# The edge stage of a graph-attention kernel: nine products and nine additions in each of the last eight turns with logits, and one turn without logits at the end instead of two

## The chip, the cores and the metric

The kernel runs on one core of a Trainium2 chip. A core has five engines, each with its own stream of instructions: TensorE (PE, whose weight loads are listed as PEld), VectorE (DVE), ScalarE (ACT), GpSimd (POOL) and SyncE (SP). They meet only at semaphores. The metric is the device time of one execution in microseconds (us); lower is better. A q behind an engine's name (DVEq) stands for its sequencer, which handles register loads and semaphore waits and hands the rest to the engine.

## What is computed

One layer on 6250 nodes of 256 features: a layer norm, graph attention with 8 heads over 100000 edges sorted by destination, a residual, then a second norm and a mixture of 16 experts (top 2). The change touches only the attention's sum over edges:

```
h = jnp.einsum('ni,hio->hno', x, W)
attn_src = jnp.einsum('hno,ho->hn', h, a_src[..., 0])
attn_dst = jnp.einsum('hno,ho->hn', h, a_dst[..., 0])
edge_attn = jax.nn.leaky_relu(attn_src[:, src] + attn_dst[:, dst], negative_slope=0.2)
edge_attn_exp = jnp.exp(edge_attn - jnp.max(edge_attn))
attn_sum = jax.ops.segment_sum(edge_attn_exp.T, dst, num_segments=N)
attn_norm = edge_attn_exp / (attn_sum[dst].T + 1e-10)
weighted_h = attn_norm[..., None] * h[:, src]
out = jax.ops.segment_sum(weighted_h.transpose(1, 0, 2), dst, num_segments=N)
```

## The kernel before

There are four stages. The first norms the nodes, projects them and stores rows of 264 numbers (256 features and 8 source logits) in `node_rows`. The second is the edge stage, from about 100 to 1194 us. The third divides by the sums, adds the residual, norms again and routes tokens to experts. The fourth runs the experts and the last norm.

In the edge stage the edges lie in 832 steps of up to 128 edges, each step's edges within one tile of 128 destination nodes. Eight steps are a group (`GROUP`), so there are 104 groups (`GROUPS`). For each step POOL issues one indirect gather of 128 rows of `node_rows` (L773), into one of four slots of eight steps. Everything else of the stage is a software pipeline in turns, `for g in range(GROUPS + 2)`, which PE and DVE each write out in their own program:

- In a turn g below 104 ("with logits") DVE forms the logits of group g: it sums four parts of the destination logits that PE put into a bank (`edge_logits_sum`, L1311), adds the gathered source logits once the group's rows have landed (`edge_logits_add`, L1318: the z addition), applies the slope, and takes a maximum over heads and steps (L1329, `zmax`). PE transposes `zmax` (L935), DVE reduces it and updates the running maximum (L1334, L1336), PE spreads that over the partitions (L942), and ACT negates it, takes the exponentials and builds the one-hot matrices of the group's destinations. DVE then multiplies the gathered rows by them in four quarters (`weigh`, L1344).
- In a turn g from 2 on, PE forms the eight products of group g - 2 (`aggregate`, L917: a transposed one-hot times 128 rows of 264), each into one of five banks, and DVE adds each product to its tile's rows in SBUF (`add_step`, L1358; for a group's first step L1356, which also scales by `fall`). The product of step k waits for addition k - 5 (`acc_add`), and addition k waits for product k (`agg_mm`) and addition k - 1.

So turns 104 and 105 have no logits; they only sum groups 102 and 103. In turn 104 DVE also prepares the epsilons of the division (`tile_max`, L1370 to L1380), PE spreads them (L957), and in turn 105 DVE copies them out (L1383). The next stage's first instruction on DVE is L1424.

The tile of a step is data, so DVE and PE load eight tile numbers per turn into registers (`tiles_of`, one TENSOR_LOAD at L418). DVE does it at the head of its turn, ahead of `edge_logits_sum`.

## Time and profile before

| | |
|---|---|
| time before, median of 3 runs | 1827.97 us (1824.74 to 1829.16) |
| the profiled execution's own time | 1831.03 us |
| its span from first to last instruction | 1828.2 us |
| granted TensorE clock, mean over the span | 0.83 of full |
| busy: PE, DVE, ACT, POOL | 75%, 64%, 41%, 67% |
| idle of POOL before the gathers (L773) | 288.5 us, of it 219.9 us "issue" |
| last gather issued | 1167.7 us |

The span is that of one execution under the profiler, and its own time lies 2.8 us above it and 3.1 us above the median. All starts below count from the span's first instruction. In the rows "idle before" is the time for which the engine had nothing to do ahead of an instruction, and the name behind the arrow is what the profile takes for the cause of its end. "issue" means that no semaphore accounts for it.

### The profile page before, as it was taken

The numbers are of one execution on the slowest core, as the hardware profiler recorded it, in microseconds if no ns is written. First come the engines' busy times: TensorE is split into PE (matmuls) and PEld (weight loads), VectorE is DVE, ScalarE is ACT, GpSimd is POOL, SyncE is SP. The second block draws the span as 40 slices with busy tenths as digits, with TensorE's granted clock in tenths as the row PEclk, the third lists the DMA queues.
The fourth block names the chain that finished last, engine by engine and source line by source line (L and its number), as shares of the span: only waits on it lengthen the run. The fifth ranks groups of instructions, "written<-read, shape, count | busy, mean of one in ns | idle before, by whom it ended". The sixth has DMA issues, their size and how long they took to land. (4 is left out here: it accounts for less than half of the span.)

```text
span 1828.2 us, 28107 instructions
## 1 busy us (share of the span) xinstructions
PE 1376.6 (75%) x6723; PEld 1059.3 (58%) x6723; DVE 1178.4 (64%) x3565; ACT 752.0 (41%) x2240; POOL 1233.2 (67%) x1237
## 2 busy tenths in 40 slices
PE   4926767767677667767667777757689999999965
PEld 3714444444444444444444444446579999999953
DVE  6757777777777777777777777689834443333346
ACT  2624444545444444445444454434323333333335
POOL 1267777777777777777777777426547767656746
PEclk9958888888878888787788887755589999999977
DMA  7344444444444444444444444265468878888874
GB/s 230 120 136 134 130 134 130 133 130 136 129 133 134 131 132 130 135 128 133 128 127 135 130 135 136 63 218 179 117 194 225 212 205 216 215 204 206 214 187 165
DMA packets 167984, 283.80 MB, mean 155 GB/s; under 512 B 33294, under 2 KB 94822, under 8 KB 167670
## 3 DMA queue, kind: packets, MB, share of 16 engines
q0 software_dynamic: 62256, 143.99, 31.7%
q1 hardware_dynamic: 102466, 137.18, 24.1%
q10 hardware_dynamic: 3108, 0.85, 0.2%
q8 instruction: 64, 1.05, 0.2%
q14 instruction: 90, 0.74, 0.2%
HBM read 240.57 MB, written 42.16 MB: 155 GB/s over the span
## 5 line engine op out<-in xcount | busy, mean ns | idle before, releaser
L773 POOL DMA_INDIRECT region<-node_rows,region x832 | 818.3, 984 | 288.5 <-issue 219.9
L917 PE MATMUL bank<-region 128*128 128x264 f32 x1664 | 599.8, 508 | 0.7 <-DVE region L1356 0.3
L1358 DVE TENSOR_TENSOR region<-region,bank 128x264 f32 x728 | 311.0, 427 | 222.2 <-PE bank L917 209.2
L917 PEld LDWEIGHTS bank<-region 128*128 128x128 f32 x1664 | 377.5, 244 | 69.3 <-DVE region L1344 0.7
L1344 DVE TENSOR_TENSOR region<-region 128x512 f32<-128x512 f32 x416 | 285.2, 687 | 3.1 <-ACT region L645 3.1
L631 ACT ACTIVATE region<-iota_row,region 128x128 f32<-128x128 f32 x832 | 262.5, 386 | 0.0
L935 PE MATMUL bank<-ident,zmax 128*1 128x128 f32 x104 | 33.0, 318 | 301.8 <-DVE zmax L1329 301.8
L641 ACT ACTIVATE neg_max<-bank 128x1 f32<-128x1 f32 x104 | 17.8, 171 | 584.5 <-PE bank L942 584.5
L705 ACT ACTIVATE region<-bank,b_col 128x128 f32<-128x128 f32 x452 | 129.5, 368 | 306.9 <-PE bank L1050 304.2
L833 POOL DMA_INDIRECT sum_rows<-region,row_u x113 | 179.4, 1587 | 107.6 <-DVE region L1709 43.8
L1050 PEld LDWEIGHTS bank<-region 128*128 128x128 f32 x1808 | 221.2, 193 | 6.2 <-DVE region L1666 0.5
L1050 PE MATMUL bank<-region 128*128 128x128 f32 x1808 | 221.9, 276 | 0.1
L1062 PE MATMUL bank<-region 128*128 x904 | 214.1, 380 | 0.5 <-DVE region L1709 0.5
L935 PEld LDWEIGHTS bank<-ident,zmax 128*1 128x1 f32 x104 | 8.2, 79 | 348.3 <-DVE zmax L1329 348.3
L1062 PEld LDWEIGHTS bank<-region 128*128 128x128 f32 x904 | 162.9, 190 | 18.8 <-issue 1.2
L636 ACT ACTIVATE region<-region,ones 128x512 f32<-128x512 f32 x208 | 150.1, 722 | 6.8
L806 POOL DMA_INDIRECT region<-y_rows,token_u x113 | 112.4, 994 | 51.1 <-issue 24.7
L1709 DVE SCALAR_TENSOR_TENSOR region<-bank,region 128x256 f32<-128x256 f32 x113 | 54.6, 484 | 139.5 <-PE bank L1062 78.5
L1666 DVE COPY region<-bank 128x256 f32<-128x256 f32 x113 | 47.8, 423 | 124.2 <-PE bank L1039 124.2
L565 ACT ACTIVATE region<-bank 128x256 f32<-128x256 f32 (+4 forms) x182 | 65.5, 380 | 97.6 <-PE bank L980 42.1
L905 PE MATMUL bank<-attn_parts,region 128*128 x832 | 95.2, 187 | 0.6
L942 PEld LDWEIGHTS bank<-run_max,ones 1*128 1x128 f32 x208 | 47.2, 281 | 69.1 <-DVE run_max L1336 69.1
(239 smaller groups left out, 1550.1 us busy)
## 6 DMA issues: line engine op xcount, KB each, us to landing
region<-in_L_ffn_w SPq DMA_DIRECT2D x129, 512.0 KB, 5.0
region<-dloc_rows SPq DMA_DIRECT2D x104, 256.0 KB, 3.4
region<-node_rows,region POOLq DMA_INDIRECT x832
node_rows<-region SPq DMA_DIRECT2D x12, 528.0 KB, 3.1
y_rows<-region SPq DMA_DIRECT2D x7, 896.0 KB, 5.9
sum_rows<-region SPq DMA_DIRECT2D x7, 896.0 KB, 7.5
region<-in_x SPq DMA_DIRECT2D x6, 896.0 KB, 10.5
region<-sum_rows SPq DMA_DIRECT2D x5, 896.0 KB, 11.1
```

What stands on the lines that cost most here:

```text
L631: ins = s.activation(onehot[:, slot + j, :], iota_row[:, :], ACT.Square, bias=dloc[:, k:k + 1], scale=-1.0)
L636: s.activation(four, four, ACT.Relu, bias=ones[:, 0:1], scale=-1.0).then_inc(onehot_ok)
L705: ins = s.activation(hidt_buf[:, j % 2, f * P:(f + 1) * P], bank[HIDT_BANKS[j % 2]][:, f * P:(f + 1) * P], ACT.Relu, bias=flat_b1[:, bass. ...
L773: p.indirect_dma_start(gathered[g % SLOTS][:, j, :], None, node_rows, bass.IndirectOffsetOnAxis(src_idx[:, k:k + 1], 0)).then_inc(row_in[g ...
L806: p.indirect_dma_start(xg_buf[:, j % XG, :], None, y0_rows, bass.IndirectOffsetOnAxis(token_u[:, j:j + 1], 0)).then_inc(xg_in[j % XG], 16)
L833: p.indirect_dma_start(sum_rows, bass.IndirectOffsetOnAxis(row_u[:, j:j + 1], 0), y_buf[:, j % 3, :], None, compute_op=ALU.add).then_inc(y ...
L905: ins = pe.matmul(z_bank(g)[:, j * AD:(j + 1) * AD], onehot_t[:, g % 2, j, :], flat_parts[:, bass.ds(tiles[j] * AD, AD)], start=False, sto ...
L917: pe.matmul(bank[AGG_BANKS[k % AGG]][:, 0:ROW], onehot[:, (g % 3) * GROUP + j, :], gathered[g % SLOTS][:, j, :], start=True, stop=True).th ...
L1050: ins = pe.matmul(bank[HIDT_BANKS[j % 2]][:, f * P:(f + 1) * P], w1_buf[:, j % W1_SLOTS, c * HIDDEN + f * P:c * HIDDEN + (f + 1) * P], xgt ...
L1062: ins = pe.matmul(bank[Y_BANKS[j % 2]][:, 0:F_IN], hidt_buf[:, j % 2, f * P:(f + 1) * P], w2_sb[:, bass.ds(expert * (FC * F_IN) + f * F_IN ...
L1344: v.tensor_tensor(hv, hv, pv, ALU.mult).then_inc(weigh_ok)
L1358: v.tensor_tensor(rows, rows, new, ALU.add).then_inc(acc_add)
```

## The change

The steps are no longer tied to turns by `(g - 2) * GROUP`. A function `first_sum(g)` says where a turn begins: up to turn 95 as before, then one step further ahead with each of the turns 96 to 103, so that these eight turns take nine steps each, and turn 104 takes group 103. Turn 105 is gone. PE's `aggregate` and DVE's `add_step` now take step numbers. On DVE the additions come from a generator, `sums(g)`, which loads the tile numbers when its first addition is asked for, and once more for the ninth. The ninth addition stands behind the fourth quarter of `weigh`. `tile_max(3)` stands behind the seventh addition of turn 104 instead of the eighth, and `tile_max(4)` behind the last addition of all. Each product of PE names three semaphores instead of two (every fourth one did so before).

```diff
@@ -367,6 +367,15 @@
+
+        CATCH_UP = 8
+
+        def first_sum(g):
+
+            return min(STEPS, max(0, (g - 2) * GROUP + min(max(g - (GROUPS - CATCH_UP), 0), CATCH_UP)))
+
+        def sums_of(g):
+            return range(first_sum(g), first_sum(g + 1))
...
@@ -413,10 +422,10 @@
-        def tiles_of(eng, engine, g):
+        def tiles_of(eng, engine, k, n):
 
             _, tiles = nc.values_load_multi_w_load_instructions(
-                tile_row[0:1, g * GROUP:(g + 1) * GROUP], engines=[engine], min_val=0, max_val=TILES - 1,
+                tile_row[0:1, k:k + n], engines=[engine], min_val=0, max_val=TILES - 1,
                 skip_runtime_bounds_check_because="the value was clamped on chip")
             return tiles
...
-            def aggregate(g, js):
-                for j in js:
-                    k = g * GROUP + j
-                    if j % 4 == 0:
-                        pe.wait_ge(onehot_ok, 2 * g + j // 4 + 1)
-                    pe.wait_ge(weigh_ok, 4 * g + j // 2 + 1)
+            def aggregate(steps):
+                for k in steps:
+                    g, j = k // GROUP, k % GROUP
+                    pe.wait_ge(onehot_ok, k // 4 + 1)
+                    pe.wait_ge(weigh_ok, k // 2 + 1)
                     if k >= AGG:
                         pe.wait_ge(acc_add, k - AGG + 1)
                     pe.matmul(bank[AGG_BANKS[k % AGG]][:, 0:ROW], onehot[:, (g % 3) * GROUP + j, :],
@@ -922,10 +930,10 @@
-            for g in range(GROUPS + 2):
-                now, last, more = g < GROUPS, g >= 2, g + 1 < GROUPS
-                if last:
-                    aggregate(g - 2, range(0, 1))
+            for g in range(GROUPS + 1):
+                now, more = g < GROUPS, g + 1 < GROUPS
+                steps = sums_of(g)
+                aggregate(steps[0:1])
                 if now:
                     pe.wait_ge(zmax_ok, g + 1)
                     if g >= 1:
@@ -933,16 +941,14 @@
                     else:
                         pe.wait_ge(late_step, LATE["late"])
                     pe.transpose(bank[M_BANK][0:1, 0:P], zmax[:, g % 2:g % 2 + 1], ident[:, :]).then_inc(zmax_tr)
-                if last:
-                    aggregate(g - 2, range(1, 4))
+                aggregate(steps[1:4])
                 if now:
                     pe.wait_ge(run_max_ok, g + 1)
                     if g >= 1:
                         pe.wait_ge(neg_max_ok, g)
                     pe.matmul(bank[M_BANK][:, P + 8:P + 9], ones[0:1, :], run_max[:, g + 1:g + 2], start=True,
                               stop=True).then_inc(max_bc)
-                if last:
-                    aggregate(g - 2, range(4, 6))
+                aggregate(steps[4:6])
                 if more:
                     attn_dst_of(g + 1)
                 if g == GROUPS:
@@ -950,8 +956,7 @@
                     pe.wait_ge(gmax_ok, GROUPS)
                     pe.wait_ge(neg_max_ok, GROUPS)
                     pe.transpose(bank[M_BANK][0:1, 0:P], late_min[:, :], ident[:, :]).then_inc(late_mm)
-                if last:
-                    aggregate(g - 2, range(6, GROUP))
+                aggregate(steps[6:])
                 if g == GROUPS:
                     pe.wait_ge(late_step, LATE["eps_row"])
                     pe.matmul(bank[M_BANK][:, 256:256 + TILES], ones[0:1, :], eps_row[:, 0:TILES], start=True,
@@ -1343,8 +1348,8 @@
                 pv = gathered[g % SLOTS][:, js, F_IN:ROW].unsqueeze(3).broadcast_to([P, 2, HEADS, F_OUT])
                 v.tensor_tensor(hv, hv, pv, ALU.mult).then_inc(weigh_ok)
 
-            def add_step(g, j, tile):
-                k = g * GROUP + j
+            def add_step(k, tile):
+                g, j = k // GROUP, k % GROUP
                 if j == 0:
                     v.wait_ge(fall_ok, g + 1)
                 v.wait_ge(agg_mm, k + 1)
@@ -1384,34 +1389,37 @@
                     v.memset(base[:, 0, :], 0.0).then_inc(late_step)
             onehots_t(0)
             late_groups()
-            for g in range(GROUPS + 2):
-                now, last = g < GROUPS, g >= 2
-                tiles = None
-                if last:
-                    if g == 2:
-                        v.wait_ge(acc_zero, 7)
-                        v.wait_ge(table_step, TABLE["tile_row"])
-                    tiles = tiles_of(v, mybir.EngineType.DVE, g - 2)
+            def sums(g):
+
+                steps, tiles = sums_of(g), None
+                for n, k in enumerate(steps):
+                    if n % GROUP == 0:
+                        if k == 0:
+                            v.wait_ge(acc_zero, 7)
+                            v.wait_ge(table_step, TABLE["tile_row"])
+                        tiles = tiles_of(v, mybir.EngineType.DVE, k, min(GROUP, len(steps) - n))
+                    yield add_step(k, tiles[n % GROUP])
+            for g in range(GROUPS + 1):
+                now = g < GROUPS
                 if now:
                     edge_logits_sum(g)
                     edge_logits_add(g)
                     edge_logits_relu(g)
                     edge_logits_max(g)
-                for j in range(GROUP):
-                    if last:
-                        add_step(g - 2, j, tiles[j])
+                adds = sums(g)
+                for j in range(GROUP + 1):
+                    next(adds, None)
                     if now and j == 1:
                         running_max(g)
                     if j == 3 and g + 1 < GROUPS:
                         onehots_t(g + 1)
-                    if now and j >= 4:
+                    if now and 4 <= j < 8:
                         weigh(g, j - 4)
                     if g == GROUPS and j < 3:
                         tile_max(j)
-                    if g == GROUPS and j == 7:
+                    if g == GROUPS and j == 6:
                         tile_max(3)
-                    if g == GROUPS + 1 and j == 1:
-                        tile_max(4)
+            tile_max(4)
```

What this moves on the engines is shown at three places. Line numbers of the changed kernel are 5 to 9 higher here: L427 is the register load, L1361 and L1363 are the additions, L925 is the product.

The first place is DVE at the boundary of two ordinary turns, before. L1344 is the last quarter of `weigh`, L1311 to L1329 are the logits of the next turn, and L1356 is its first addition (ISA rows set up its address).

```order
L1358 TENSOR_TENSOR region<-region,bank 128x264
L1344 TENSOR_TENSOR region<-region 128x2x256
L418 TENSOR_LOAD tile_row
L1311 TENSOR_REDUCE z<-bank 128x64
L1318 TENSOR_TENSOR z<-z,region 128x64
L1323 SCALAR_TENSOR_TENSOR z<-z 128x64
L1329 TENSOR_REDUCE zmax<-z 128x1
L1356 ISA
L1356 SCALAR_TENSOR_TENSOR region<-region,fall,bank 128x264
```

The same boundary in the changed kernel:

```order
L1363 TENSOR_TENSOR region<-region,bank 128x264
L1349 TENSOR_TENSOR region<-region 128x2x256
L1316 TENSOR_REDUCE z<-bank 128x64
L1323 TENSOR_TENSOR z<-z,region 128x64
L1328 SCALAR_TENSOR_TENSOR z<-z 128x64
L1334 TENSOR_REDUCE zmax<-z 128x1
L427 TENSOR_LOAD tile_row
L1361 ISA
L1361 SCALAR_TENSOR_TENSOR region<-region,fall,bank 128x264
```

The load has moved from ahead of the logits to between `zmax` and the first addition. This is so in every turn from 2 to 103, not only in the last eight.

The second place is DVE at the boundary of turns 102 and 103 in the changed kernel, where the ninth addition and its own load stand behind the last quarter of `weigh`.

```order
L1363 TENSOR_TENSOR region<-region,bank 128x264
L1349 TENSOR_TENSOR region<-region 128x2x256
L427 TENSOR_LOAD tile_row
L1363 ISA
L1363 TENSOR_TENSOR region<-region,bank 128x264
L1316 TENSOR_REDUCE z<-bank 128x64
L1323 TENSOR_TENSOR z<-z,region 128x64
```

One addition more stands ahead of the next turn's logits.

The third place is PE from the last turn with logits on, before. L935 and L942 are turn 103's two small steps, L952 transposes `late_min`, and L957 spreads the epsilons; L980 is the next stage.

```order
L935 MATMUL bank<-ident,zmax 1x128
L917 MATMUL bank<-region 128x264 x3
L942 MATMUL bank<-run_max,ones 128x1
L917 MATMUL bank<-region 128x264 x10
L952 MATMUL bank<-ident,late_min 1x128
L917 MATMUL bank<-region 128x264 x2
L957 MATMUL bank<-eps_row,ones 128x49
L917 MATMUL bank<-region 128x264 x8
L980 MATMUL bank<-ident,region 128x128 x4
```

The same in the changed kernel:

```order
L943 MATMUL bank<-ident,zmax 1x128
L925 MATMUL bank<-region 128x264 x3
L949 MATMUL bank<-run_max,ones 128x1
L925 MATMUL bank<-region 128x264 x11
L958 MATMUL bank<-ident,late_min 1x128
L925 MATMUL bank<-region 128x264 x2
L962 MATMUL bank<-eps_row,ones 128x49
L985 MATMUL bank<-ident,region 128x128 x4
```

The eight products behind the epsilons are gone, one product more stands ahead of L958, and the spreading of the epsilons is now PE's last work of the stage.

## Rows read from the trace of the kernel before

**Rows 1.** Instructions on node_rows: durations (ns min/median/max), starts; idle before, by releaser (us, times)

```profile
L773 POOL DMA_INDIRECT region<-node_rows,region x832: 942/946/2137, 97.5 to 1167.7; - x167
...
  issue: 219.9, 722
...
  PE bank L917: 33.2, 109
```

**Rows 2.** Waits from 150 to 1190: who <- whom: us in total, times, longest

```profile
DVE z L1318 <- DMA region<-node_rows,region: 54.7, 84, 2.4
```

**Rows 3.** DVE, z additions of turns 98-101, 103: start, length (us) [idle before]

```profile
1118.91 0.23 DVE L1318 TENSOR_TENSOR z<-z,region 128x64 f32<-128x64 f32 x1 [1.38 <-DMA region<-node_rows,region]
...
1129.55 0.23 DVE L1318 TENSOR_TENSOR z<-z,region 128x64 f32<-128x64 f32 x1
...
1139.16 0.22 DVE L1318 TENSOR_TENSOR z<-z,region 128x64 f32<-128x64 f32 x1 [0.39 <-DMA region<-node_rows,region]
...
1149.92 0.23 DVE L1318 TENSOR_TENSOR z<-z,region 128x64 f32<-128x64 f32 x1
...
1171.80 0.23 DVE L1318 TENSOR_TENSOR z<-z,region 128x64 f32<-128x64 f32 x1 [1.42 <-DMA region<-node_rows,region]
```

**Rows 4.** Timeline of DVE from the end of turn 103 to the next stage

```profile
1179.71 0.42 DVE L1358 TENSOR_TENSOR region<-region,bank 128x264 f32 x1
1180.05 0.69 DVE L1344 TENSOR_TENSOR region<-region 128x512 f32<-128x512 f32 x1
1180.66 0.48 DVE L1356 SCALAR_TENSOR_TENSOR region<-region,fall,bank 128x264 f32 x1
...
1185.55 0.43 DVE L1358 TENSOR_TENSOR region<-region,bank 128x264 f32 x1 [0.21 <-DVE region L1358]
1185.90 0.27 DVE L1380 TENSOR_SCALAR eps_row<-bank 1x128 f32<-1x128 f32 x1
...
1189.43 0.20 DVE L1383 COPY eps_bc<-bank 128x49 f32<-128x49 f32 x1
...
1193.86 0.22 DVE L1424 TENSOR_TENSOR rsum<-region,eps_bc 128x56 f32<-128x56 f32 x1
```

**Rows 5.** Timeline of PE, the broadcast of the epsilons

```profile
1186.22 0.66 PE L957 MATMUL bank<-eps_row,ones 1*128 1x49 f32 x2 [1.12 <-DVE eps_row L1380]
```

**Rows 6.** The register load L418 on DVE: all of them, then one

```profile
L418 DVEq TENSOR_LOAD <-tile_row x104: 593/596/859, 123.9 to 1185.6; - x104
...
L418 DVEq TENSOR_LOAD <-tile_row x1: 593/593/593, 1157.4 to 1157.4; - x1
```

**Rows 7.** Timeline of DVE, the start of turn 102

```profile
1160.47 0.23 DVE L1318 TENSOR_TENSOR z<-z,region 128x64 f32<-128x64 f32 x1 [1.50 <-DMA region<-node_rows,region]
...
1160.99 0.22 DVE L1329 TENSOR_REDUCE zmax<-z 128x1 f32<-128x64 f32 x1
1161.22 0.49 DVE L1356 SCALAR_TENSOR_TENSOR region<-region,fall,bank 128x264 f32 x1
...
1162.73 0.43 DVE L1358 TENSOR_TENSOR region<-region,bank 128x264 f32 x1 [1.02 <-PE bank L917]
```

**Rows 8.** Timeline of DVE, the first two additions of turn 101

```profile
1150.67 0.49 DVE L1356 SCALAR_TENSOR_TENSOR region<-region,fall,bank 128x264 f32 x1
...
1151.64 0.43 DVE L1358 TENSOR_TENSOR region<-region,bank 128x264 f32 x1 [0.48 <-PE bank L917]
```

**Rows 9.** Timeline of DVE, start of turn 88, and the z addition of turn 89

```profile
1015.54 0.23 DVE L1318 TENSOR_TENSOR z<-z,region 128x64 f32<-128x64 f32 x1 [0.29 <-DMA region<-node_rows,region]
...
1016.64 0.49 DVE L1356 SCALAR_TENSOR_TENSOR region<-region,fall,bank 128x264 f32 x1 [0.36 <-issue]
1017.80 0.43 DVE L1358 TENSOR_TENSOR region<-region,bank 128x264 f32 x1 [0.67 <-PE bank L917]
...
1025.73 0.23 DVE L1318 TENSOR_TENSOR z<-z,region 128x64 f32<-128x64 f32 x1 [0.34 <-DMA region<-node_rows,region]
```

**Rows 10.** The semaphore instruction ahead of each product, L916, on PE's sequencer

```profile
L916 PEldq EVENT_SEMAPHORE  x827: 51/51/51, 134.1 to 1190.4; - x166
```

More of the change, by code:

```diff
@@ L900, in attn_dst_of @@
                     pe.wait_ge(z_sum, g - 1)
-                tiles = tiles_of(pe, mybir.EngineType.PE, g)
+                tiles = tiles_of(pe, mybir.EngineType.PE, g * GROUP, GROUP)
                 pe.matmul(z_bank(g), ones_b[:, :], far_row[:, :, :, :].rearrange("a j k h -> a (j k h)"),
```

## Prediction

> **What bounds the kernel now.** I read the gathers first, then DVE's waits, then the timeline at the stage's end. The reader should see that in the edge stage POOL sets the pace, and that behind the last gather DVE sets the end.
>
> The 832 gathers start from 97.5 to 1167.7, one each 1.288 us, so a turn of eight takes 10.30 us. A gather is at work for 946 ns, and the idle time before it is 0.30 us, whether it is put down to "issue" (219.9 / 722) or to PE's products (33.2 / 109) [rows 1]. Had a slot ever come free late, the second kind would be longer. So no gather waited for a product, and an earlier product brings the gathers nothing.
>
> DVE's z addition waits for rows in 84 of some 100 turns, 54.7 us together [rows 2], or 0.55 us a turn. DVE's own work in a turn is thus 10.30 - 0.55 = 9.75 us. This 0.55 us is all that an ordinary turn can take in unseen. What is unused in one turn can't be saved for a later one, but a delay in one is made up in the next ones.
>
> Turn 103 starts with an idle 1.42 us, at 1171.80 [rows 3]: the last rows set that moment. From there on nobody waits for POOL. The fourth quarter of weigh starts at 1180.05, turn 104's additions at 1180.66, and the next stage's L1424 follows without idle time at 1193.86 [rows 4]. All that comes later hangs on that instruction, so what is gained here is gained at the end.
>
> **The change part by part.**
>
> *The end, 1180.66 to 1193.86, now 13.20 us [rows 4].* In its place there will be:
> - The ninth addition of turn 103, in the slot in which turn 104 starts now. The next addition can't start before it is finished: 0.43 us long plus 0.21 us of hand-over, as in the row at 1185.55 [rows 4]. That is 0.64 us.
> - Turn 104's eight additions with the same steps of tile_max between them: from the first to the eighth 1185.55 - 1180.66 = 4.89 us [rows 4]. PE may run four products ahead, and its rows of group 103 were weighed a turn ago, so I let the spacing stand.
> - The epsilons. L1380 starts 0.35 us after the addition ahead of it (1185.90 - 1185.55) [rows 4], which is now the seventh, 0.64 us ahead of the eighth. PE's broadcast starts 0.32 us later and lasts 0.66 us (1186.22) [rows 5]. The copy takes 0.20 us [rows 4]. I estimate 0.1 us for each of the two hand-overs behind these. From the seventh addition to L1424 that makes 0.35 + 0.32 + 0.66 + 0.1 + 0.20 + 0.1 = 1.73 us, or 1.09 us from the eighth. Today the copy at 1189.43 is covered by additions. That cover is gone, and this is its price.
>
> That is 0.64 + 4.89 + 1.09 = 6.62 us in place of 13.20: **6.58 us saved.**
>
> *The register load, moved in every turn.* Today it stands behind the fourth quarter of weigh: the load at 1157.4 takes 0.593 us beside DVE's running work [rows 6] and costs nothing. In the new place it starts when zmax has been handed to DVE, which then holds 0.22 us of work. The first addition follows zmax by 0.23 us today (1160.99, 1161.22) [rows 7]; it can now come 0.6 us later (0.596 median of 104 loads [rows 6], plus a few hundredths). What hides it: the second addition waits for PE's product, whose way starts at zmax and not at the first addition. Needed between the two additions is 0.49 + 0.21 = 0.70 us. Turn 102 has 1162.73 - 1161.22 = 1.51 us, so 0.81 us of cover and no cost [rows 7]. Turn 101 has 1151.64 - 1150.67 = 0.97 us, so 0.27 us of cover, and 0.6 costs 0.35 us [rows 8]. The trace has tried it: in turn 88 the first addition came 0.36 us late, the second 1.16 us behind it, and the turn's work was 1025.73 - 0.34 - 1015.54 = 9.85 us, no more than turn 102's 1171.80 - 1.42 - 1160.47 = 9.91 [rows 3, 7, 9]. Either price fits under 0.55 us a turn. In turn 103, where there is no cover behind, I charge the dearer: **0.35 us lost.** Bounds: 0 to 0.6.
>
> The Trainium skill speaks against this part: its page "Runtime: NRT & Kernel Launch", section Instruction fetch mechanics, gives a TENSOR_LOAD about 200 ns per register even in bulk. Eight registers would by that take 1.6 us, 0.8 more than turn 102's cover, and the sum would be a slower kernel. The load's rows contradict it, and the rows decide.
>
> *The ninth addition and its load in turns 96 to 102.* Behind a quarter of weigh an addition shifts what follows by 0.34 us (1179.71 to 1180.05) [rows 4]; the bound above is the 0.64 of two additions in a row. Its load of one register takes between nothing and the 0.6 us of eight, and runs beside weigh as the load at 1157.4 does. Does this fit? A turn starts at the later of its rows and the end of the turn before. Turn 98's work, 1129.55 - 1118.91 = 10.64, plus 0.34, makes turn 99 start at 1129.89 instead of 1129.55. Turn 99 (9.22 + 0.34 + 0.35) ends at 1139.80, 0.64 late. Turn 100 (10.76 + 0.34) ends at 1150.90, 0.98 late. Turn 101 (9.05 + 0.34 + 0.35) ends at 1160.64, 0.17 late. Turn 102 (9.91 + 0.34) ends at 1170.89, still 0.91 us before the rows of turn 103 [rows 3, 7]. **Cost 0**, with 0.9 us to spare; up to 2 us when the slow turns fall last.
>
> *PE's third wait.* There is one semaphore instruction of 51 ns ahead of each product, 827 in all, the same for products that name two semaphores and for those that name three [rows 10]. The third adds none: 0. At most it would be another 0.05 us in a turn's first product. The ninth product of a turn stands ahead of PE's wait for zmax, so it is hidden.
>
> **Sum:** 6.58 - 0.35 = **6.2 us**. The profiled execution, 1831.03, would become 1824.8 and its span 1822.0. The median of the runs lies 3.1 us under it: 1827.97 - 6.2 = **1821.8 us**, 0.34% faster. About 0.3% (5.5 us, a time of 1822.5) is what a measurement can tell from no change, so the forecast lies barely past it.
>
> **The rivals.**
>
> 1. *DVE late in turn 103.* Nine steps use nearly all the slack of a turn of 10.30 us. If turns like 98 and 100 (10.6 to 10.8 us) are the last ones, two of them with 0.34 more each lose 2 x 0.8 us against POOL (10.76 + 0.34 - 10.30), and only some of the usual 0.55 us can be set against it. For: turns 98 to 101 are such a cluster. Against: turn 102 makes it up with 0.9 to spare. The gain shrinks by 1 to 2 us: 1823 to 1824, within 0.3%.
> 2. *Slower: the load is not hidden.* If the late first addition delays PE's transposition or the whole turn by its full 0.6 us, DVE's work becomes 9.75 + 0.62 = 10.37 > 10.30 and DVE takes the lead. Stepping through all turns as above, with 0.62 in each and 0.34 more in the last ones, makes turn 103 start 12.6 us late: 1821.8 + 12.6 = 1834.4. It is slower by 0.3% once turn 103 is 11.7 us late, that is, from 0.6 us uncovered in every turn. Against it: turn 88. For it: turn 88 was late by 0.36, not 0.6. At 0.4 uncovered, the lag is 1.1 us and the result within 0.3%.
> 3. *The gain is given back or never seen.* The last stretch depends on PE's clock (granted at two levels, and 0.83 on average), and the three runs spread over 4.4 us. A half-clock stretch in turn 104, where products would have to pass additions, costs 1 to 3 us: 1823 to 1825.
> 4. *More than forecast.* PE at full clock through the epsilons saves about 0.3, and the load in turn 103 under cover 0.35; with the scatter of runs, 1819 to 1821.
>
> **How the numbers follow.** The forecast has 0.57, rival 1 0.15, rival 2 0.08 (over half of it slower by more than 0.3%), rival 3 0.12, rival 4 0.08. The forecast's own range is 1820 to 1824, from the bounds 0 to 0.6 for the load and a run's scatter of 1.5 us. To hold 8 in 10 it takes in rival 1 and most of 3 and 4: 1819.0 to 1826.0. Faster by over 0.3%: 0.7 of the forecast and nearly all of rival 4, with a little of 1 and 3, 0.52. Within 0.3%: the rest of these and part of 2, 0.40. Slower: 0.08.
>
> **What would show it.** In the changed kernel's timeline: the last gather near 1168 and turn 103's z addition near 1172, with some idle time ahead of it (step: no lag); the first addition 0.8 us behind zmax instead of 0.23, and the second at most 0.35 us later than before; the ninth addition 0.34 us long in its slot; no second block of eight additions; the copy of the epsilons behind the last addition with about 0.5 us of idle time; the next stage's first instruction 15.8 us after turn 103's z addition instead of 22.06 (1193.86 - 1171.80). The prediction is wrong if the z waits vanish (rival 2), if the z addition of turn 103 has no idle time (rival 1), or if additions in turn 104 wait for products (rival 3).

## The result: 8 us slower, and the profile after

Six runs of each kernel gave a median of 1836.55 us (1831.42 to 1841.31) after the change and 1828.57 us (1824.74 to 1829.86) before it. The ratio is 1.0044 [1.0026, 1.0062]: slower, on the side to which the prediction gave 0.08, 15 us from the predicted time and outside the range of 1819.0 to 1826.0. Two repetitions, on chips where the kernel before took 1828 and 1831 us, gave 1.0043 and 1.0034.

The gathers first, once as the list of all instructions on `node_rows`, once as groups of instructions from 90 to 1190 us (busy us, mean ns | idle before, by releaser):

```profile
L782 POOL DMA_INDIRECT region<-node_rows,region x832: 945/949/2114, 98.0 to 1177.2; - x167
...
L782 POOL DMA_INDIRECT region<-node_rows,region x832 | 826.8, 994 | 288.5 <-issue 221.3 <-DMA node_rows<-region 35.2 <-PE bank L925 32.0
```

The last gather starts 9.5 us later than in [rows 1]. POOL's idle time is the same 288.5 us and its pattern is the same, so the gathers wait no more than before. The gathers themselves take longer: 8.5 us more in all, while the median has hardly moved (949 against 946 ns). The kernel before has this row in the same view:

```profile
L773 POOL DMA_INDIRECT region<-node_rows,region x832 | 818.3, 984 | 288.5 <-issue 219.9 <-DMA node_rows<-region 35.4 <-PE bank L917 33.2
```

A mean of 984 ns over a median of 946 means that some gathers were already much longer than 946 ns before. The prediction read only the median.

Next the z additions of DVE in turns 97 and 99 to 103:

```profile
1117.39 0.23 DVE L1323 TENSOR_TENSOR z<-z,region 128x64 f32<-128x64 f32 x1 [0.44 <-DMA region<-node_rows,region]
...
1140.57 0.22 DVE L1323 TENSOR_TENSOR z<-z,region 128x64 f32<-128x64 f32 x1
...
1151.99 0.23 DVE L1323 TENSOR_TENSOR z<-z,region 128x64 f32<-128x64 f32 x1
...
1162.33 0.23 DVE L1323 TENSOR_TENSOR z<-z,region 128x64 f32<-128x64 f32 x1
...
1173.84 0.23 DVE L1323 TENSOR_TENSOR z<-z,region 128x64 f32<-128x64 f32 x1
...
1185.37 0.23 DVE L1323 TENSOR_TENSOR z<-z,region 128x64 f32<-128x64 f32 x1
```

From turn 98 on none waits for rows, and the turns take 11.4 to 11.6 us instead of 10.3; only turn 100 (1151.99 to 1162.33) takes 10.34. Turn 103 starts 8.2 us after the last gather's start, before it was 1171.80 - 1167.7 = 4.1 [rows 1, 3]. What happens inside turn 102, and the register loads of DVE (all 111; then those of turn 102, of turn 100, and one of a single register):

```profile
1174.36 0.22 DVE L1334 TENSOR_REDUCE zmax<-z 128x1 f32<-128x64 f32 x1
...
1176.47 0.43 DVE L1363 TENSOR_TENSOR region<-region,bank 128x264 f32 x1 [1.88 <-PE bank L925]
```

```profile
L427 DVEq TENSOR_LOAD <-tile_row x111: 308/596/1867, 132.0 to 1195.0; - x111
...
L427 DVEq TENSOR_LOAD <-tile_row x1: 1866/1866/1866, 1174.4 to 1174.4; - x1
...
L427 DVEq TENSOR_LOAD <-tile_row x1: 606/606/606, 1152.5 to 1152.5; - x1
...
L427 DVEq TENSOR_LOAD <-tile_row x1: 308/308/308, 1172.1 to 1172.1; - x1
```

The profile puts the 1.88 us down to PE, but the load that starts at 1174.4 lasts until 1176.3, and the addition behind it starts then. A load of eight registers takes 1.85 to 1.87 us where its first step is 761, 770, 779, 797, 806 or 815, and 0.60 us where it is 752, 788 or 824. The latter are multiples of four; of these only 788, in turn 100, isn't also a multiple of eight. Until turn 96 every first step is one of eight.

In an ordinary turn, here turn 87, the new place of the load does to DVE what the prediction said: the first addition 0.87 us behind `zmax` instead of 0.23, the second 0.70 behind that.

```profile
1011.88 0.22 DVE L1334 TENSOR_REDUCE zmax<-z 128x1 f32<-128x64 f32 x1
1012.75 0.49 DVE L1361 SCALAR_TENSOR_TENSOR region<-region,fall,bank 128x264 f32 x1 [0.65 <-issue]
1013.45 0.43 DVE L1363 TENSOR_TENSOR region<-region,bank 128x264 f32 x1 [0.21 <-PE bank L925]
```

The end of the stage, from the ninth addition of turn 103 on, answers to [rows 4]:

```profile
1195.23 0.42 DVE L1363 TENSOR_TENSOR region<-region,bank 128x264 f32 x1
1195.90 0.49 DVE L1361 SCALAR_TENSOR_TENSOR region<-region,fall,bank 128x264 f32 x1 [0.24 <-PE bank L925]
...
1200.45 0.43 DVE L1363 TENSOR_TENSOR region<-region,bank 128x264 f32 x1
...
1200.93 0.21 DVE L1388 COPY eps_bc<-bank 128x49 f32<-128x49 f32 x1
...
1201.18 0.22 DVE L1432 TENSOR_TENSOR rsum<-region,eps_bc 128x56 f32<-128x56 f32 x1
```

From turn 103's z addition to the next stage it is 1201.18 - 1185.37 = 15.81 us instead of 22.06. The spans then differ thus: 9.5 us until the last gather's start, 8.2 - 4.1 = 4.1 until turn 103, -6.25 in the end stretch, and 2.4 behind it (636.7 against 634.3 us, work that the change doesn't touch; 636.4 and 636.8 in two more profiles of the changed kernel, and 634.7 to 637.8 in the variants below on chips as fast). Together 9.7, as 1837.9 - 1828.2.

### The profile page after: what moved, and what is told of

It reads as the page before. It is cut to its first block and busy times, and to the rows that moved or that the text cites. A ratio compares the mean times of both kernels' runs of the same rounds, so it can differ in the third digit from the quotient of the medians.

```text
span 1837.9 us, 28117 instructions
## 1 busy us (share of the span) xinstructions
PE 1393.5 (76%) x6723; PEld 1068.3 (58%) x6723; DVE 1177.0 (64%) x3565; ACT 751.8 (41%) x2240; POOL 1244.2 (68%) x1237
## 3 DMA queue, kind: packets, MB, share of 16 engines
q8 instruction: 64, 1.05, 0.2%
## 5 line engine op out<-in xcount | busy, mean ns | idle before, releaser
L782 POOL DMA_INDIRECT region<-node_rows,region x832 | 826.8, 994 | 288.5 <-issue 221.3
L925 PE MATMUL bank<-region 128*128 128x264 f32 x1664 | 615.9, 519 | 0.2
L925 PEld LDWEIGHTS bank<-region 128*128 128x128 f32 x1664 | 387.4, 250 | 71.3 <-issue 0.3
L1363 DVE TENSOR_TENSOR region<-region,bank 128x264 f32 x728 | 310.9, 427 | 175.1 <-PE bank L925 152.5
L650 ACT ACTIVATE neg_max<-bank 128x1 f32<-128x1 f32 x104 | 17.8, 171 | 598.6 <-PE bank L949 598.6
L1055 PEld LDWEIGHTS bank<-region 128*128 128x128 f32 x1808 | 220.9, 193 | 6.2 <-DVE region L1674 0.5
L1067 PEld LDWEIGHTS bank<-region 128*128 128x128 f32 x904 | 162.9, 190 | 20.0 <-issue 2.5
L1361 DVE SCALAR_TENSOR_TENSOR region<-region,fall,bank 128x264 f32 x104 | 50.9, 489 | 66.4 <-issue 63.4
```

The source lines that it names most:

```text
L782: p.indirect_dma_start(gathered[g % SLOTS][:, j, :], None, node_rows, bass.IndirectOffsetOnAxis(src_idx[:, k:k + 1], 0)).then_inc(row_in[g ...
L925: pe.matmul(bank[AGG_BANKS[k % AGG]][:, 0:ROW], onehot[:, (g % 3) * GROUP + j, :], gathered[g % SLOTS][:, j, :], start=True, stop=True).th ...
L1055: ins = pe.matmul(bank[HIDT_BANKS[j % 2]][:, f * P:(f + 1) * P], w1_buf[:, j % W1_SLOTS, c * HIDDEN + f * P:c * HIDDEN + (f + 1) * P], xgt ...
L1067: ins = pe.matmul(bank[Y_BANKS[j % 2]][:, 0:F_IN], hidt_buf[:, j % 2, f * P:(f + 1) * P], w2_sb[:, bass.ds(expert * (FC * F_IN) + f * F_IN ...
L1363: v.tensor_tensor(rows, rows, new, ALU.add).then_inc(acc_add)
```

## The experiments

**Theory A:** the load's new place costs time in every turn, and the first steps that are no multiples of four cost time in the last ones; without both the change brings its 6 us. **Rival B:** nine steps in a turn are too many for DVE or PE, whatever the loads do. **Rival C:** one of the two suspects is the whole loss.

### Each suspect alone and both

`load_ahead`: the changed kernel with the load back ahead of the logits; the first steps stay.

```diff
+                tiles = first_tiles(g)
                 if now:
                     edge_logits_sum(g)
...
-                adds = sums(g)
+                adds = sums(g, tiles)
```

`load_by_group`: the changed kernel, but the tile numbers are loaded a whole group of eight at a time, when its first is needed; the place stays.

```diff
+                n = k // GROUP
+                if n not in group_tiles:
+                    group_tiles[n] = tiles_of(v, mybir.EngineType.DVE, n * GROUP, GROUP)
+                return group_tiles[n][k % GROUP]
```

`both`: that, and the groups needed for the turn's first eight steps are loaded ahead of its logits.

```diff
             for g in range(GROUPS + 1):
                 now = g < GROUPS
+                for k in sums_of(g)[:GROUP]:
+                    tile_of(k)
```

`before_moved`: the kernel before, with eight steps a turn, and nothing but the load moved.

```diff
-                if last:
-                    tiles = tiles_of(v, mybir.EngineType.DVE, g - 2)
                 if now:
                     edge_logits_sum(g)
                     edge_logits_add(g)
                     edge_logits_relu(g)
                     edge_logits_max(g)
+                if last:
+                    tiles = tiles_of(v, mybir.EngineType.DVE, g - 2)
```

The first time:

> The changed kernel with its register load back ahead of the logits in every turn; in turns 97 to 103 it still begins at the turn's own first step. Two costs are supposed: the load's place (P) makes the gathers longer, so the last one ends 9.2 us later than before; the load's start (S), off a multiple of four, makes it 1.86 us instead of 0.60 and puts turn 103 another 4.4 us behind its rows. If P holds: last gather back near 1169, time 1828.6 - 6.2 + what S still costs behind weigh (0 to 5) = 1822.4 to 1827.5. Rival (the gathers' delay has another cause: scatter, or PE's third wait): last gather still near 1178, time 1831 to 1836.

> The changed kernel, but DVE loads eight tile numbers per group, always from a multiple of eight, at the group's first addition; in ordinary turns that is the same place as in the changed kernel. If S holds: every load 0.6 us, turn 103 no longer late against its rows, 4.4 us less than the changed kernel's 1836.5: about 1832. P stays, so the last gather stays near 1178. Rival (the lag at turn 103 comes from the ninth addition, not from the load): no change from 1836.5.

> The kernel before with one thing changed: the register load stands between zmax and the first addition, always eight from a multiple of eight. If P holds: weigh falls differently against the gathers, the last gather ends some 3 to 9 us later, time 1831.5 to 1838. Rival (place costs nothing, as I predicted): 1828.6 within 1.5.

> The changed kernel with loads of whole groups, ahead of the logits: both supposed costs gone, the nine additions and the missing turn kept. If P and S are all that was wrong: the predicted gain, 1828.6 - 6.6 = 1822.0 (1820.5 to 1824). If nine steps a turn cost something of their own: 1825 or more.

Measured: 1.0022 [1.0009, 1.0034], 0.9974 [0.9958, 0.9989], 0.9990 [0.9979, 1.0001] and 0.9995 [0.9984, 1.0007]. They tell little of this result, for the kernel before took 2026.67 us on that chip, 11% more than on the first. The granted clock was 0.77 to 0.79 there, against 0.81 to 0.83 on the first. POOL's waits there look like this (`both`, 150 to 1360 us):

```profile
POOL region L782 <- PE bank L925: 156.4, 135, 6.9
```

PE's products, up to 6.9 us late, held the gathers back. So POOL alone didn't set the pace of the edge stage there. The four were run again, on a chip where the kernel before took 1831.71 us, and the changed kernel as it is on another, where the kernel before took 1827.94:

> The changed kernel itself, beside the kernel before, on the chip that the next experiments may get. On a chip where the kernel before takes about 1828: 1833 to 1841, the last gather near 1178. Where the kernel before takes about 2027, as on the chip of the first four experiments, PE and DVE and not the gathers set the pace of the turns (z addition idle 0.03 in every turn); there each misaligned load of 1.86 costs its whole excess of 1.26 in six turns and the place of the load up to 0.35 a turn: 2027 - 6.2 + 7.6 = 2028 or more.

> The kernel of e1 again, hoped to run on a chip where the kernel before takes about 1828 and the gathers set the pace. The changed kernel's load is back ahead of the logits, still misaligned in six turns. P (the load's place makes the gathers longer, by 5 to 9 us at the last one) and S (the load's start, off a multiple of four, puts turn 103 about 6 us behind its rows). If P holds: last gather as early as in the kernel before (1169), and a time of 1828.3 - 6.2 + 0 to 5 for S = 1822 to 1827. Rival (the gathers' delay has another cause): last gather at 1172 to 1178 and 1828 or more.

> The kernel of e2 again. The load's place as in the changed kernel, but always eight numbers from a multiple of eight. If S holds: 0.6 us each, turn 103 starts 2 to 3 us behind its last gather instead of 7 to 8, and the time is 5 to 6 less than the changed kernel's: 1829.5 to 1831. Rival (the lag comes from the ninth addition): about 1835.5.

> The kernel of e3 again: the kernel before with the load moved between zmax and the first addition and nothing else. If P holds: last gather 3 to 9 us later than in the kernel before, 1831.5 to 1837. Rival (place costs nothing where the gathers set the pace, as I predicted): 1828.3 within 1.5.

> The kernel of e4 again: nine products and additions, turn 105 gone, loads of whole groups ahead of the logits. If P and S are all that was wrong: 1828.3 - 6.6 = 1821.7 (1820 to 1824). If nine steps a turn cost something of their own: 1825 or more.

| kernel | place of the load | first steps | ratio to before |
|---|---|---|---|
| as changed (again) | behind zmax | as in the change | 1.0043 [1.0024, 1.0061] |
| load_ahead | ahead of logits | as in the change | 1.0008 [0.9994, 1.0022] |
| load_by_group | behind zmax | multiples of eight | 0.9994 [0.9981, 1.0007] |
| both | ahead of logits | multiples of eight | 0.9974 [0.9957, 0.9990] |
| before_moved | behind zmax | multiples of eight, no ninth step | 1.0033 [1.0016, 1.0050] |

Both suspects cost time, and without them the change gains 0.26%: A holds and B falls. C falls because `before_moved`, with the place alone, is slower than the kernel before, and because the intervals of `load_ahead` and `both`, which differ in the first steps alone, don't meet. The place costs 0.33% by itself (6.0 us), 0.20% between `load_by_group` and `both`. The first steps cost 0.34% between `load_ahead` and `both` (6.2 us), and 0.4 to 0.5% between `as changed` and `load_by_group`. These last differences between kernels are a good deal less certain than each ratio. In `before_moved` DVE doesn't set the pace: it waits for rows in 75 turns between 150 and 1190 us, 50.9 us together, and turn 103's z addition waits 1.20 us. It is the gathers that are longer, as after the change:

```profile
L773 POOL DMA_INDIRECT region<-node_rows,region x832 | 826.1, 993 | 288.6 <-issue 216.0 <-PE bank L917 37.2 <-DMA node_rows<-region 35.4
...
1180.03 0.23 DVE L1318 TENSOR_TENSOR z<-z,region 128x64 f32<-128x64 f32 x1 [1.20 <-DMA region<-node_rows,region]
```

The gathers' own evidence is weaker than the times. Between the starts of gathers 40 and 768 (counted from 0), in turns where all kernels sum eight steps and load from multiples of eight, the profiles give 942.1 to 946.0 us with the load behind `zmax` (five profiles), and 935.6 (before), 939.0, 939.2 (`both`) and 942.2 (`load_ahead`) with it ahead of the logits. The last gather of `load_ahead` starts at 1174.7, not near 1169 as was expected if the place lengthens the gathers, and its time fell on the side of the rival, 0.08% above the kernel before. `load_ahead` and `both` run the same instructions in those turns, so 3 us of it are scatter from profile to profile. In the repeated changed kernel the last gather starts at 1171.3, where 1178 was expected. `load_by_group` came out some 2 us better than expected (0.9994 of 1828.3 is 1827.2); `before_moved` and `both` fell within what was expected of them.

### What makes a gather longer

In the timeline of the changed kernel a long gather lies beside DVE's `weigh`, whose two operands (rows and weights) both come from SBUF:

```profile
168.39 0.69 DVE L1349 TENSOR_TENSOR region<-region 128x512 f32<-128x512 f32 x1
168.52 1.38 POOL L782 DMA_INDIRECT region<-node_rows,region  x1 [0.30 <-PE bank L925]
...
169.33 0.69 DVE L1349 TENSOR_TENSOR region<-region 128x512 f32<-128x512 f32 x1
...
170.20 0.95 POOL L782 DMA_INDIRECT region<-node_rows,region  x1 [0.30 <-issue]
```

In the kernel before, a gather that starts ahead of `weigh` keeps its length, and one that starts behind it doesn't:

```profile
619.27 0.95 POOL L773 DMA_INDIRECT region<-node_rows,region  x1 [0.30 <-issue]
...
619.40 0.69 DVE L1344 TENSOR_TENSOR region<-region 128x512 f32<-128x512 f32 x1
...
620.34 0.69 DVE L1344 TENSOR_TENSOR region<-region 128x512 f32<-128x512 f32 x1
...
620.52 1.32 POOL L773 DMA_INDIRECT region<-node_rows,region  x1 [0.30 <-issue]
```

Counted over its whole timeline from 150 us on, all 47 gathers that start 0.05 to 0.35 us behind the start of a `weigh` take 1.15 to 1.44 us, and all 127 that start 0.05 to 0.45 us ahead of one take 0.94 to 1.01. A gather that meets a `weigh` at work thus seems to be held until about its end.

`weigh_psum` takes the second operand from a PSUM bank instead. What is in that bank isn't the weights, so this kernel and the next leave the attention weights out of `weigh`; size and form stay. `weigh_psum_moved` moves the load as well. **Theory:** the load's place costs time only by shifting `weigh` against the gathers. **Rival:** it costs time through DVE itself.

```diff
-                pv = gathered[g % SLOTS][:, js, F_IN:ROW].unsqueeze(3).broadcast_to([P, 2, HEADS, F_OUT])
+                pv = bank[M_BANK][:, 256:256 + 2 * HEADS].rearrange("p (j h) -> p j h", h=HEADS).unsqueeze(3).broadcast_to(
+                    [P, 2, HEADS, F_OUT])
```

> The kernel before, but weigh multiplies the gathered rows by 16 numbers that lie in a PSUM bank (the tfirst row) instead of by the attention weights in SBUF: same shape, one operand less read from SBUF, output not the reference's. Theory C (a gather that is at work while weigh reads two operands from SBUF is held until it ends, which costs 0.3 us a turn): all gathers take 0.95 us, last gather after 1070 - 30 = 1040 us from the first if DVE keeps up, time 1800 to 1812. Rival (the long gathers have nothing to do with weigh's operands): gathers as long as before (mean 0.98), time 1828 within 2.

> The same, with the register load between zmax and the first addition in every turn (the kernel of e7 with weigh's second operand in PSUM). If the load's place costs time only through C, by where weigh falls against the gathers: same time as e9 within 0.15%. Rival (the load's place costs DVE's own time, 0.1 us a turn, that the gathers hide): with the gathers faster the turns hang on DVE and it shows: 5 to 15 us slower than e9.

> The changed kernel on the same chip and in the same rounds as e11: 1.0044 of the kernel before (1.003 to 1.006).

> The kernel of e8 again, beside the changed kernel: 0.9965 of the kernel before if the end's 6.6 us is all there is, 0.9974 by e8; against r2 it should be 11 to 14 us faster.

These four fell on a chip where the kernel before takes 2053.33 us: 1.0097 [1.0076, 1.0118], 1.0095 [1.0060, 1.0129], 0.9989 [0.9976, 1.0003] and 0.9974 [0.9962, 0.9986]. Again POOL waited for products there (`weigh_psum`, 150 to 1400 us), so shorter gathers bring nothing, and the first two were slower than the kernel before, where a clear gain was expected of `weigh_psum`, for a cause that was not looked for:

```profile
POOL region L773 <- PE bank L917: 192.0, 126, 7.8
```

The same on a chip where the kernel before takes 1831.35 us:

> The kernel of e9 again (before, with weigh's second operand in PSUM), hoped for on a chip where the kernel before takes about 1830. On the slow chip it had no gather above 1.1 us but for one, so theory C stands for the gathers' length. If the gathers also set the time: mean gather 0.948 instead of 0.981, 832 x 0.033 = 27 us less by the last one if DVE keeps up, but DVE's own 9.75 us a turn with PE's clock leaves only 0.25 of idle time in 10.0: 1802 to 1815. Rival (turns then hang on DVE): 1815 to 1828.

> The kernel of e10 again (the same with the load between zmax and the first addition). If the load's place costs only by where weigh falls against the gathers: within 0.15% of e12. Rival (it costs DVE's own time, 0.1 us a turn): 3 to 10 us slower than e12.

> The changed kernel in the same rounds as e14: 1.0044 of the kernel before.

> The kernel of e8 in the same rounds as r3: 0.9965 to 0.9974 of the kernel before, 11 to 14 us faster than r3; turn 103's z addition at most 3 us behind its last gather's end, against 7 to 8.5 in r3.

Measured: 0.9853 [0.9834, 0.9873], 0.9858 [0.9838, 0.9877], 1.0034 [1.0018, 1.0050], 0.9974 [0.9957, 0.9991]. The gathers of `weigh_psum` and of `weigh_psum_moved`, and how long DVE's z addition waited for rows in each:

```profile
L773 POOL DMA_INDIRECT region<-node_rows,region x832 | 793.5, 954 | 287.0 <-issue 217.0 <-PE bank L917 36.3 <-DMA node_rows<-region 33.7
...
DVE z L1318 <- DMA region<-node_rows,region: 39.7, 60, 1.8
```

```profile
L773 POOL DMA_INDIRECT region<-node_rows,region x832 | 793.0, 953 | 288.8 <-issue 213.4 <-PE bank L917 39.9 <-DMA node_rows<-region 35.5
...
DVE z L1318 <- DMA region<-node_rows,region: 17.8, 28, 1.5
```

The mean gather falls from 984 to 954 ns, which is 24.8 us of the 26.9 that the kernel gains. In `weigh_psum` 100 gathers start 0.05 to 0.35 us behind the start of a `weigh`, and all take 0.94 to 0.95 us, as this one:

```profile
662.05 0.68 DVE L1345 TENSOR_TENSOR region<-region,bank 128x512 f32<-128x512 f32 x1
...
662.26 0.95 POOL L773 DMA_INDIRECT region<-node_rows,region  x1 [0.30 <-issue]
```

So this contention has a price of some 25 us, and the kernel before paid it already. Without it the load's place costs 0.05%. DVE does lose about 22 us of slack to the load (39.7 - 17.8), 0.22 us a turn and so within the 0 to 0.35 that the prediction let it lose, and the kernel loses next to nothing by that. So the theory holds: the place costs through the gathers. How many gathers meet a `weigh` in its first 0.05 to 0.35 us fits this, but doesn't prove it by itself: 47 in the kernel before, 60, 64 and 75 in the other profiles with the load ahead of the logits, and 65 to 83 in the five with it behind `zmax`. Of the expectations one more missed: `both` was 9.6 us faster than the changed kernel by the medians, where 11 to 14 were expected.

### A version that beats both

`p_in_psum` is `both`, with the full computation: ACT takes the exponentials twice, into SBUF for PE's products and into a PSUM bank for `weigh`.

```diff
+                s.activation(p_bank(), z[:, g % 2, :, :], ACT.Exp, bias=neg_max[:, g + 1:g + 2]).then_inc(p_ok)
...
-                pv = gathered[g % SLOTS][:, js, F_IN:ROW].unsqueeze(3).broadcast_to([P, 2, HEADS, F_OUT])
+                pv = p_bank()[:, js, :].unsqueeze(3).broadcast_to([P, 2, HEADS, F_OUT])
```

> A whole kernel built on what e12 and e14 showed: e14's form (nine products and additions in the last eight turns, group loads ahead of the logits), and ACT takes the exponentials twice, into SBUF for PE's products and into a PSUM bank, from which weigh reads its second operand. The second exponential (0.35 us on ACT) delays weigh only where it falls ahead of its first quarter's slot. Theory C: 0.9853 of the kernel before as e12, less 0.003 for the end, plus lag in the nine-step turns, which now have only 0.25 us of slack each: 0.982 to 0.988, 1799 to 1810 where the kernel before takes 1831. Rival (the exponential's delay puts DVE past 10.03 us a turn): 0.99 or more.

It took 1798.54 us against 1830.73: 0.9817 [0.9793, 0.9842], a little better than the range expected. The second ACT instruction costs 0.30 us, the gathers take 953 ns, and `weigh`, now with an operand from a bank, takes no longer than before:

```profile
1030.92 0.30 ACT L660 ACTIVATE bank<-z,neg_max 128x64 f32<-128x64 f32 x1
...
1031.56 0.68 DVE L1354 TENSOR_TENSOR region<-region,bank 128x512 f32<-128x512 f32 x1
...
L787 POOL DMA_INDIRECT region<-node_rows,region x832 | 793.0, 953 | 287.9 <-issue 212.7 <-PE bank L930 40.5 <-DMA node_rows<-region 34.8
```

## Why the prediction was wrong

**Right: the end.** Forecast 15.8 us from turn 103's z addition to the next stage, measured 15.81. That the number is exact is luck, for sizes in it were off and cancel. From the ninth addition on it is 1201.18 - 1195.23 = 5.95 us, where 6.62 was forecast: the eight additions take 4.55 instead of 4.89, and the epsilons 0.73 instead of 1.09. Turn 103 up to there takes 9.86 us instead of 8.86 + 0.35 = 9.21, because of its slow load. `both` without it takes 1183.92 - 1175.24 = 8.68 (its own row here):

```profile
1175.24 0.22 DVE L1323 TENSOR_TENSOR z<-z,region 128x64 f32<-128x64 f32 x1 [0.37 <-DMA region<-node_rows,region]
...
1183.92 0.42 DVE L1363 TENSOR_TENSOR region<-region,bank 128x264 f32 x1
```

**Right: the ninth step and PE's third wait.** With `both`, nine steps a turn, turn 103 still waits for its rows, 0.37 us, and the kernel gains 0.26% twice: 4.8 us, where the prediction's terms without the load's 0.35 give 6.58, which lies within the interval (1.8 to 7.9 us). From turn 103's z addition to the next stage it needs 14.6 us, less than forecast. What it doesn't gain stands ahead of that: its last gather starts 1073.9 us behind the first, against 1070.2 before. Whether that is scatter or comes from the nine steps or the third wait, no run separates. The semaphore instruction ahead of a product still takes 51 ns in the median with three waits for each:

```profile
L924 PEldq EVENT_SEMAPHORE  x827: 51/51/606, 134.8 to 1198.4; - x166
```

**The first step that failed: "A gather is at work for 946 ns", and with it "Either price fits under 0.55 us a turn" as all that the load's place costs.** The gathers were taken as fixed, at the median of 946 ns, and the load's cost was sought only in DVE's slack. The slack did hold it. But shifting DVE's work against POOL's changes how long gathers take: 3.7 to 6 us, of which nothing stood in the sum. The prediction's own numbers showed that something was missing: 0.946 + 0.30 makes 1.246 us, eight of them 9.97, and a turn takes 10.30. That the engines meet only at semaphores, as the first section has it, is not so either: POOL's gathers get longer by what DVE does, without a semaphore between them.

The Trainium skill, "SBUF — State Buffer", section Who interferes with whom, says that a DVE instruction with two SBUF inputs contends with a GpSimd instruction that reads SBUF. The fall from 984 to 954 ns agrees with that. It also says that in a probe `tensor_tensor` did not seem to stall a DMA, and infers that making descriptors needs only the write side of the shared ports. Here it does lengthen the instruction that issues an indirect gather, and the measurement decides. Which of that instruction's accesses is held, no run here shows.

**The second step that failed: "0.596 median of 104 loads" as the price of every load of eight.** All 104 rows were of loads that begin at a multiple of eight. Of the eight at the head of the turns with nine steps, six begin elsewhere and take 1.86 us, 1.05 more than the 0.81 us of cover found in turn 102. Those turns take 11.4 to 11.6 us instead of 10.3, turn 103 is about 4 us late behind its rows, and 1.2 us longer in itself: 5.3 us by the profile, 6.2 by `load_ahead` against `both`. In `load_ahead` too DVE waits for it, 1.25 us ahead of the logits:

```profile
1185.28 0.42 DVE L1316 TENSOR_REDUCE z<-bank 128x64 f32<-128x256 f32 x1 [1.25 <-issue]
```

The prediction set aside a rule of the Trainium skill ("Runtime: NRT & Kernel Launch", Instruction fetch mechanics: about 200 ns per register) because the rows spoke against it. The page has loads from HBM in mind, and `tile_row` lies in SBUF. For the loads from multiples of four the rows do speak against it, 0.60 / 8 = 0.075 us a register; for the six others 1.86 / 8 = 0.23 us comes near it. The rows of before held no such load, so they could not decide for these.

Put together: -4.8 for what the change is for, 3.7 to 6.0 for the place, 6.2 to 9 for the first steps give 5 to 10 us; measured 8.0. These terms come from ratios of the same runs, so the sum is no test by itself. Rival 2 came out near the time (1834.4), but not by its mechanism: DVE did not take the lead in ordinary turns, as 78 waits for rows of up to 1.8 us show:

```profile
DVE z L1323 <- DMA region<-node_rows,region: 48.1, 78, 1.8
```

Rival 1's sign, no idle time ahead of turn 103's z addition, showed too, but not by rival 1's mechanism either: `both` has the nine steps and keeps the idle time; what used it up were the slow loads.

**Left open.** That the multiple of four decides is read from nine starting steps, not tried by itself, and 788 is the only one that tells four from eight. The stretch from the first gather's start to the last's scatters by some 4 us between profiles of one kernel (1075.4, 1075.9 and 1079.2 after the change), so the split between place and first steps is no finer than that. Why two chips took 11 to 12% longer was not found; the granted clock on them was 0.76 to 0.79 against 0.80 to 0.84 on the others, and no run shows whether that is the cause.

## What to carry to other kernels

Where the engine that sets the pace shows a mean well above its median, find out what lengthens the long ones before moving anything beside it: here one operand in PSUM brought 26.9 us, where the change at its best brought 4.8. A duration is only priced for the addresses and shapes that the trace has; if a change alters where a load begins, bound it by the dearest reading, not by the rows of the old form. Slack on an engine says what a shift costs that engine, not what it costs its neighbours.

## What the runs showed of the hardware

- A load of eight registers on DVE from SBUF took about 0.60 us (0.59 to 0.61, once 0.86) where its first element was a multiple of eight or, in one case, of four, and 1.85 to 1.87 us from the others; one register took 0.31 us.
- A 128x512 multiplication on DVE with both operands in SBUF lengthens an indirect gather on POOL that starts 0.05 to 0.35 us behind it, to 1.15 to 1.44 us instead of 0.95. With one operand in PSUM 100 such gathers took 0.94 to 0.95, and gathers that started 0.05 to 0.45 us ahead of it took at most 1.01 anyway. The multiplication's own time doesn't show it (0.69 against 0.68 us with one operand in PSUM).
- The same kernel took 1828 to 1832 us on at least three chips, and 2027 and 2053 us on two others. On the slow ones gathers waited up to 7.8 us for PE's products, and comparisons came out with the other sign: the two kernels with `weigh`'s operand in PSUM clearly (1.01 instead of 0.985), the changed kernel and `before_moved` by 0.1% and within their intervals.
